# First steps of the pipeline reordered: normalisation ahead of the keys' rounding, zero fills by GpSimd, constants and the second pair's key work behind the maxima

## The reference

```python
xn = layernorm(x)                               # no affine part
scores = einsum(q=xn, k=ctx) / 4                # 16 heads; causal and padding mask
x = x + tanh(g_xattn) * (softmax(scores) @ ctx_heads @ W.T + b)
x = x + tanh(g_ffn) * ffn(layernorm(x))         # shared SwiGLU, then 8 experts in 2 groups, top 2
```

## Time and profile before

| | us |
|---|---|
| median of 3 runs | 1137.24 (1136.03 to 1137.77) |
| the profiled execution's own time | 1135.77 |
| its span, first to last instruction | 1134.1 |
| PE busy | 1067.0 (94%) |
| DVE busy | 851.0 (75%) |
| POOL busy | 514.0 (45%) |
| ACT busy | 471.8 (42%) |

### The profile page before, as it was taken

How to read it: one execution, slowest core, us unless ns; L and a number is a source line. 1 busy time by engine, 2 the same in 40 slices (tenths; PEclk the granted TensorE clock), 3 DMA queues, 4 the chain that set the end, 5 groups by cost and what they waited for, 6 DMA issues and landing times.

```text
span 1134.1 us, 22176 instructions
## 1 busy us (share of the span) xinstructions
PE 1067.0 (94%) x7283; PEld 901.5 (79%) x7283; DVE 851.0 (75%) x1863; ACT 471.8 (42%) x722; POOL 514.0 (45%) x613
## 2 busy tenths in 40 slices
PE   3769999999999999999999999999999999999997
PEld 2557888888788788788888877888887888888886
DVE  7768888897987887987888666557454688888886
ACT  3546556556556555565555522233221111111111
POOL 4234447448357366465373624000001566666564
PEclk8889999999999999999999999999999899999999
DMA  6795657747656665765666112687652554555451
GB/s 134 147 226 137 139 95 161 148 111 129 147 127 127 131 134 135 120 156 129 105 125 135 45 47 83 207 268 232 213 173 99 166 160 150 164 167 151 149 174 64
DMA packets 108129, 161.84 MB, mean 143 GB/s; under 512 B 29100, under 2 KB 72942, under 8 KB 108016
## 3 DMA queue, kind: packets, MB, share of 16 engines
q1 hardware_dynamic: 96244, 122.40, 46.0%
q0 software_dynamic: 11776, 38.03, 11.1%
HBM read 76.43 MB, written 52.12 MB: 113 GB/s over the span
## 4 chain that ended last, share of the span: by engine, by line
PE 80%; DVE 9%; issue 3%; DMA 3%; ACT 2%; SPq 2%; POOL 1%; POOLq 0%; ACTq 0%; DVEq 0%
PE ps L773 16%; PE ps L718 12%; PE ps L820 12%; PE ps L735 7%; PE ps L822 6%; PE ps L628 4%; PE ps L640 4%; PE ps L671 3%; PE ps L805 3%; PE ps L593 3%; PE ps L649 2%; PE ps L623 1%; PE ps L694 1%; DVE mneg L1229 1%; DMA regr<-regr 1%
## 5 line engine op out<-in xcount | busy, mean ns | idle before, releaser
L820 PE MATMUL ps<-regr,gh 128*128 x600 | 221.0, 406 | 0.1
L897 ACT ACTIVATE Pt<-ps,pbias 77x1024 f32<-77x1024 f32 x128 | 141.5, 1105 | 100.0 <-PE ps L628 98.7
L822 PE MATMUL ps<-regr,gl 128*128 x600 | 169.7, 283 | 0.0
L1419 POOL TENSOR_TENSOR gl<-gf,gh 128x512 fp32r<-128x512 f32 x64 | 82.6, 1291 | 115.8 <-ACT gh L859 115.5
L820 PEld LDWEIGHTS ps<-regr,gh 128*128 128x128 f32 x600 | 113.5, 189 | 23.8 <-issue 0.7
L987 ACT ACTIVATE gh<-ps 128x512 fp32r<-128x512 f32 x75 | 44.8, 599 | 204.9 <-PE ps L805 204.9
L1229 DVE TENSOR_REDUCE mneg<-ps 128x8 f32<-128x616 f32 x128 | 100.0, 791 | 21.7 <-PE ps L593 15.8
L822 PEld LDWEIGHTS ps<-regr,gl 128*128 128x128 f32 x600 | 113.7, 189 | 0.0
L718 PE MATMUL ps<-x2h,winh 128*128 128x512 f32 x256 | 109.8, 429 | 0.5 <-DVE OHR L1102 0.5
L718 PE MATMUL ps<-x2h,winl 128*128 128x512 f32 x256 | 102.5, 400 | 0.0
L718 PE MATMUL ps<-x2l,winh 128*128 128x512 f32 x256 | 102.2, 399 | 0.0
(11 more groups left out here) (208 smaller groups left out, 2702.5 us busy)
## 6 DMA issues: line engine op xcount, KB each, us to landing
regr<-regr SPq DMA_DIRECT2D x96, 256.0 KB, 5.9
y_dram<-Pt SPq DMA_DIRECT2D x64, 256.0 KB, 2.1
regf<-in_x SPq DMA_DIRECT2D x32, 256.0 KB, 2.9
x<-in_x SPq DMA_DIRECT2D x32, 256.0 KB, 3.8
y_dram<-res SPq DMA_DIRECT2D x32, 256.0 KB, 2.4
regr<-regr SPq DMA_DIRECT2D x96, 77.0 KB, 5.9
x_dram<-x2h SPq DMA_DIRECT2D x14, 512.0 KB, 3.0
x_dram<-x2l SPq DMA_DIRECT2D x14, 512.0 KB, 3.8
```

The lines of the kernel that those rows point to most:

```text
L820: e.matmul(o, gh2[:, k % 3, fc, :], w2v[:, bass.ds(val, 1), fc, :, :].rearrange("p o h d -> p (o h) d"), start=fc == 0, stop=False, skip_g ...
L822: m = e.matmul(o[:, 0, :], gl2[:, k % 3, fc, :], w2v[:, bass.ds(val, 1), fc, 0, :].rearrange("p o d -> p (o d)"), start=False, stop=fc == ...
L897: e.activation(Pt[0:K, 4 * k:4 * k + 4, :].rearrange("k (n j) t -> k n (j t)", n=2), bank_of["sc", b, k][0:K, :, :], ACT.Exp, bias=pbias[: ...
L1419: e.tensor_tensor(gl[:, fc, :], gf[:, n % 2, :], gh[:, fc, :].bitcast(F), ALU.subtract).then_inc(s["gl"], 1)
```

## The change

Nothing is computed differently and no DMA is added or dropped. Four things are done:

- In step 0 the stage `kv` of pair 0 moves behind `norm`, so ACT normalises batch 0 before it rounds the keys, and both parts of `keys` go to slot 3.
- The zero fills of `Kst` (both halves) and of `Vau` move from DVE to POOL. Pair 0's fill is issued ahead of the loop, `Vau` at `norm` of batch 0, pair 1's fill in step 1.
- The stage `table` (marks for the DRAM table) moves from slot 5 to 9 of step 0, the fills of constants (`init`) to the end of step 1, the gates and constants (`gates`) from slot 10 to 4 of step 1.
- `pick` and `kv` of pair 1 move from steps 0 and 1 to slots 4 and 5 of step 2, behind the maxima of batch 1; those of pair 2 from step 3 to slots 4 and 5 of step 4. `keys` of batches 2 and 4 move to slot 7, and `keys` of batch 1 waits for the maxima of batch 0. The spread of pair 1 moves behind the load into `x1`.

```diff
     order += [("load_x", 0, 0), ("load_masks", 0, 0), ("load_kv", 0, 0), ("load_x", 1, 0), ("consts", 0, 0), ("moments", 0, 0),
-              ("marks", 0, 0), ("pick", 0, 0), ("kv", 0, 0)]
+              ("marks", 0, 0), ("pick", 0, 0)]
...
-        put(i, ((1, "keys", 0), (3, "keys", 1)))
+        put(i, {0: ((3, "keys", 0), (3, "keys", 1)), 2: ((7, "keys", 0), (7, "keys", 1)),
+                4: ((7, "keys", 0), (7, "keys", 1))}.get(i, ((1, "keys", 0), (3, "keys", 1))))
         if i == 0:
-            slots[5].append(("table", 0, 0))
-            slots[5].append(("init", 0, 0))
+            slots[2].append(("kv", 0, 0))
             slots[8].append(("vau", 0, 0))
-            slots[9].append(("own", 0, 0))
-            slots[11].append(("load_kv", 1, 0))
+            slots[9] += [("table", 0, 0), ("own", 0, 0)]
         if i == 1:
+            slots[4] += [("gates", 0, 0), ("load_kv", 1, 0)]
             slots[8].append(("own", 1, 0))
-            slots[10].append(("gates", 0, 0))
+            slots[9] += [("ks1", 0, 0), ("init", 0, 0)]
         if i == 2:
-            slots[4].append(("zeros", 0, 0))
+            slots[6].append(("zeros", 0, 0))
...
         if i % 2 == 1 and i + 1 < NB:
-            slots[9].append(("pick", i // 2 + 1, 0))
-            slots[11] += [("kv", i // 2 + 1, 0), ("vau", i // 2 + 1, 0)]
+            if i > 4:
+                slots[9].append(("pick", i // 2 + 1, 0))
+                slots[11].append(("kv", i // 2 + 1, 0))
+            slots[11].append(("vau", i // 2 + 1, 0))
+        if i in (2, 4):
+            slots[4].append(("pick", i // 2, 0))
+            slots[5].append(("kv", i // 2, 0))
...
                 if stage_ == "kv":
                     e.wait_ge(s["khi"], b + 1)
                     e.tensor_tensor(klo[:, :, :], kf[:, :, :], khi[:, :, :].bitcast(F), ALU.subtract).then_inc(s["klo"], 1)
-                    if b == 0:
-                        e.memset(Kst[0:96, 0, :, :, :, :].bitcast(F), 0.0).then_inc(s["dcon"], 1)
                 elif stage_ == "init":
-                    e.memset(Vau[:, :, :, :, :], 0.0).then_inc(s["dcon"], 1)
-                    e.wait_ge(s["dcon"], DCON["va_zero"])
-                    e.memset(Vau[:, :, :, :, 16:17], 1.0).then_inc(s["dcon"], 1)
...
-                elif stage_ == "zeros":
-                    e.memset(Kst[0:96, 1, :, :, :, :].bitcast(F), 0.0).then_inc(s["dcon"], 1)
...
+            e.memset(Kst[0:96, 0, :, :, :, :].bitcast(F), 0.0).then_inc(s["gcon"], 1)
+
             for stage_, b, k in order:
                 h = b % 2
-                if stage_ == "vau":
+                if stage_ == "norm" and b == 0:
+                    e.memset(Vau[:, :, :, :, :], 0.0).then_inc(s["gcon"], 1)
+                    e.wait_ge(s["gcon"], GCON["va_zero"])
+                    e.memset(Vau[:, :, :, :, 16:17], 1.0).then_inc(s["gcon"], 1)
+                elif stage_ == "ks1":
+                    e.memset(Kst[0:96, 1, :, :, :, :].bitcast(F), 0.0).then_inc(s["gcon"], 1)
+                elif stage_ == "vau":
...
+                        if b == 1:
+                            e.wait_ge(s["mlo"], 1)
```

More of the change, by code:

```diff
@@ L38 @@
 DCON = {n: i + 1 for i, n in enumerate(
-    "idb m8 ks0 va_zero va_one ones rec pre_zero pre wgh0 lb0 tgh brow pbias crow kcol ks1".split())}
-GCON = {n: i + 6 for i, n in enumerate("ident caus cauT upb kint ramp".split())}
+    "idb m8 tgh brow pbias crow kcol ones rec pre_zero pre wgh0 lb0".split())}
+GCON = {n: i + 6 for i, n in enumerate("ident caus cauT upb kint ramp ks0 va_zero va_one ks1".split())}
 ROUTES = [(4 * c - 4, 8, c) for c in range(1, NCH - 2, 2)] + [(4 * c, 4, c) for c in (NCH - 2, NCH - 1)]
@@ L480, in sync @@
                     if b == 0:
-                        e.wait_ge(s["dcon"], DCON["ks0"])
+                        e.wait_ge(s["gcon"], GCON["ks0"])
                     if b >= 2:
@@ L487, in sync @@
                     e.wait_ge(s["klo"], 2)
-                    e.wait_ge(s["dcon"], DCON["ks1"])
+                    e.wait_ge(s["gcon"], GCON["ks1"])
                     spread_kv(1)
@@ L1445, in gpsimd @@
             e.iota(ramp, pattern=[[-1, K]], base=K, channel_multiplier=0).then_inc(s["gcon"], 1)
+            e.memset(Kst[0:96, 0, :, :, :, :].bitcast(F), 0.0).then_inc(s["gcon"], 1)
             for stage_, b, k in order:
                 h = b % 2
-                if stage_ == "vau":
+                if stage_ == "norm" and b == 0:
[5 more added lines that the diff above has]
+                elif stage_ == "vau":
                     e.wait_ge(s[f"vf{h}"], 16 * (b // 2 + 1))
                     if b == 0:
-                        e.wait_ge(s["dcon"], DCON["va_one"])
+                        e.wait_ge(s["gcon"], GCON["va_one"])
                     if b >= 2:
```

## The result

The changed kernel takes 1133.97 us (median of 11 runs, 1132.08 to 1134.67), the kernel before on the same chip 1136.46 us (11 runs, 1134.78 to 1137.77). The ratio is 0.9976, 95% interval 0.9967 to 0.9985: 2.5 us less, just beyond the 0.2% (2.3 us) that the prediction called the bound of what can be told. The forecast was 0.9 us less, within the bound. 1134.0 lies in the range of 1132.6 to 1139.2, but outside the forecast's own bounds of 1135.1 to 1137.5; the direction, faster by over 0.2%, had been given 0.31.

A forecast was written before the change was run, and what follows sets the result against it. The prediction took SP and the DMA engines to bound the kernel up to 65 us, then ACT, DVE and PE in turn, and PE after the start. -3.1 + 2.2 = -0.9 us took the median 1137.24 to 1136.3 us, range 1132.6 to 1139.2.

The forecast's parts named there:

- The frame: Whole kernel: PE bounds what follows the start, so savings before about 100 us move the end by the same amount.
- Part 1: Step 0: SP's first spread starts 1.9 us earlier, at 9.55, with POOL filling at 0.8 ns per element.
- The two slower rivals: Step 0: POOL fills at 1.2 ns, 1140.1 us; or POOL's product takes the port first, 1138.7 us; chance 0.1 each.
- Part 2: Steps 1 and 2: batch 1's maxima come earlier, but SP waits for their DMA behind a table fill; -3.1 us.
- The rival of a short wait: Step 2: the maxima's DMA does not queue behind the fill, lands 3 us after issue; 1133.0 us, chance 0.2.
- The term -3.1: Up to batch 2's maxima landing: everything waiting for SP moves 3.1 us earlier, bounds -3.6 and -2.6.
- Part 3: Step 4: the pick of pair 2 is no longer free and delays batch 2's last `exp`; +2.2 us, bounds 1.5 and 2.9.
- The rival that step 4 costs little: Step 4: the slipping `exp` has slack behind it, costing 0.3 us instead of 2.2; 1134.4 us, chance 0.1.
- the two terms: SP's queue up to batch 2's maxima landing, -3.1 us, and the pick of pair 2 in step 4, +2.2 us.

The follow-up runs named there:

- fill0_dve: The changed kernel with the first fill of the stacked keys back on DVE, behind `klo`: 1143.85 us, ratio 1.0002 to the kernel before.
- x1_ahead: The kernel before with the load into `x1` ahead of pair 1's spread (pair 1's key fill moved too, unintended): 1149.88 us, ratio 1.0060 to the kernel before.
- pick2_alone: The kernel before with only pair 2's pick, rounding and values moved into step 4: 1144.72 us, ratio 1.0010 to the kernel before.
- pick2_back: The changed kernel with pair 2's key work back at the end of step 3: 1140.69 us, ratio 0.9967 to the kernel before.
- again: The changed kernel unaltered, profiled and timed a second time: 1142.36 us, ratio 0.9980 to the kernel before.

## Why the prediction was nearly right

**The frame held.** Every edit moved the start: the leads at step 5 of 0.2 and 1.6 us are still 0.2 and 1.6 us at step 7. Behind it the first pair of profiles, on one chip, moved apart by 1.0 us more, most likely by where the stretches at 1.2 GHz fell (the kernel before has one at 541 us that the changed kernel's profile lacks). The forecast sum was -0.9 us; the runs say -2.5 (here) and -2.3 (second chip).

**Part 1, right.** The spread starts at 9.29, 2.2 us earlier instead of 1.9; without it the landing of batch 1's maxima comes 0.5 to 2.2 us later and the time is 2.5 us longer, with intervals that overlap (`fill0_dve`). The two slower rivals (POOL fills at 1.2 ns; the product takes the port first) fall at the same rows: 0.87 ns, and `klo` was first by 0.14 us.

**Part 2, right in its wait and its size, wrong in its reason.** Reductions at 21.34 (22 forecast), the DMA issued at 28.53 (29), landing at 36.97 and 35.25 (35.7), and then SP's wait. The rival of a short wait (landing 3 us after the issue) falls. Its figure is the right one for that DMA with empty queues, 3.1 us (`x1_ahead`), but the queues are not empty. The failed step is that the table fill is what stands ahead: without it the landing stays at 35.25. Which of the transfers ahead of it holds it was not isolated. The term -3.1 measured -2.65 in the first pair of profiles and -4.8 in the second (64.82 to 60.03), -3.7 in the mean; the upper one lies outside the bounds of -3.6 and -2.6. The bounds took no account of the landing's scatter from one execution to the next.

**Part 3, right in what slips, not settled in size.** The last `exp` comes 1.6 us later by the first pair, 2.6 us by the second (7.7 to 10.2 behind the landing), against 2.2 forecast. The reductions of step 5 come 2.5 to 3.2 us later, since two things join that `exp`, which their rows show: POOL's product holds the normalisation L1265 from 0.73 to 1.84 us, which the prediction had only in its upper bound, and PE is granted 1.2 GHz behind its 2.7 us of waiting, which it did not have at all. In the second pair that is above the upper bound of 2.9. In time the pick costs 1.1 us (`pick2_alone`) to 1.7 us (`pick2_back`), and neither is clear of nothing. Whether the rest comes back is not settled. In `pick2_back` the clock falls in step 5 instead: the reductions of step 5 are 1.69 us ahead of `again`, and the first of step 7 only 0.72. In `pick2_alone` all of it is still there at step 7, 3.2 us. The rival that step 4 costs little named slack behind the `exp`; the rows of step 5 refute that, but its time, 0.3 us for the pick, is not excluded.

**The sum.** By the rows of step 5 the two terms were -2.65 + 2.5 = -0.2 us in the first pair and -4.8 + 3.2 = -1.6 us in the second: -3.7 + 2.8 = -0.9 us in the mean, just the forecast. That is luck, since each term was some 0.6 us larger than forecast and a single landing scatters by 2 us. The time says -2.5 and -2.3. With the cost of the pick as the times have it (1.4 us, the middle of 1.1 and 1.7) the sum would be -3.7 + 1.4 = -2.3, but that sets a landing beside two differences that are not clear of noise. So the mechanism is the one forecast, but for the fill, and the way the time went was seen; why it went 1.5 us further than the rows of step 5 is not shown. That was enough to cross a bound of 0.2%.

**What was missed.** The prediction took the change as a whole and did not ask what its first part alone would do. In time it does as much as the whole (-2.4 us against -2.3 and -2.5). By the rows of one profile the edits of step 0 by themselves tip `klo` of pair 1 ahead of POOL's copy and bring step 5 to 75.36, where the whole change reaches 77.95; 1.4 us of that lead are left at step 7. The early maxima of Part 2 pay only if the load into `x1` does not stand between them and the spread; moved behind, the same change gives 6.3 to 7.2 us instead of 2.3. The prediction named the wait and priced it against before, but not against the order in which it would not exist.

## What to carry to other kernels

When a change puts an instruction that waits ahead of issues that don't need to wait, price the wait against the same change without it, not only against the kernel before: one slot in SP's order was here worth 3.5 us in the rows and 4 to 5 us in time, more than the whole change gave. Before costing an edit from one pair of profiles, take a second pair, for here a landing behind a full queue moved by up to 1.7 us and the rest of the start with it. And where a DVE instruction with two inputs and a GpSimd instruction are ready within 0.1 us of each other, count both outcomes, since here 2.7 us hung on which was first.

## What the runs showed that was not expected

- **Stretches at 1.2 GHz drown small gains.** The shortest lasted 3.4 us (the profiles name them by the granted clock of 0.50). Two, at some 880 to 890 us and at the very end, are in every profile; most of the others lie at other places in each execution, and the count in a profile went from 5 to 9. One of 3.4 us over matmuls that PE was running back to back cost 1.4 us, over half of the bound that the prediction used. It stands at 541 us in the kernel before and is missing from the changed kernel's profile; between the same two matmuls the one took 7.90 us and the other 6.50. The 16 matmuls of L645 took 1.07 us at 2.4 GHz and 1.93 at 1.2.

```profile
539.49 0.53 PE L593 MATMUL ps<-regr 128*128 128x308 f32 x2 [1.76 <-DVE mneg L1229]
...
547.39 0.45 PE L593 MATMUL ps<-regr 128*128 128x308 f32 x2
```

```profile
538.94 0.53 PE L598 MATMUL ps<-regr 128*128 128x308 f32 x2 [1.76 <-DVE mneg L1227]
...
545.44 0.45 PE L598 MATMUL ps<-regr 128*128 128x308 f32 x2
```

- **A step made faster can hand its stretch at 1.2 GHz to the next one.** In `pick2_back` it followed an idle time of 2.03 us in step 5, and in the changed kernel one of 2.72 us in step 4. This is seen in one profile of `pick2_back`.
- **POOL fills at 0.87 ns per element**: 2464 in 2.14 us, 2048 in 1.79 us, as fast as DVE's 0.86 in the earlier trace rows.
- **A 32 KB DMA** (the maxima's) took 3.1 us alone, 6.6 to 8.4 us behind the transfers of steps 0 and 1, and 11.3 to 13.2 us behind weights and fill.
- **DVE instructions with one tensor as input were held by POOL's product as well**: L1265 took 1.84 us instead of 0.73 in step 4, L1173 1.29 instead of 0.36 in step 1. The product, by its row above, runs from 71.68 to 74.42, and L1265 ended at 74.57, 0.15 us behind it; L1173 (from 17.60) ended at 18.89, 0.15 us behind a product that ran from 17.52 to 18.74.
